# Two transformer blocks with cross-attention on one core: where the maxima's rows, the split of the feed-forward weights, the gate's first fills and the end's transfers stand

## What is computed

```python
h1 = ln(x);  x = attn(h1, h1, q1, k1, v1) @ o1 + x
h2 = ln(x);  x = attn(h2, context, q2, k2, v2) @ o2 + x     # 1601 context tokens
h3 = ln(x);  a, g = split(h3 @ ff_w1 + b1)
x = (a * gelu(g)) @ ff_w2 + b2 + x
```

## Time and profile before

| | |
|---|---|
| median of 3 runs | 3553.37 us (3542.58 to 3559.33) |
| profiled execution | 3536.07 us |
| its span of instructions | 3534.3 us |
| PE busy | 3118.4 us (88%) |
| DVE, ACT, POOL busy | 58%, 54%, 18% |
| granted clock of PE, mean | 0.936 |

### The profile page before, as it was taken

How to read it: one execution, slowest core, us unless ns; L and a number is a source line. 1 busy time by engine, 2 the same in 40 slices (tenths; PEclk the granted TensorE clock), 3 DMA queues, 4 the chain that set the end, 5 groups by cost and what they waited for, 6 DMA issues and landing times.

```text
span 3534.3 us, 43638 instructions
## 1 busy us (share of the span) xinstructions
PE 3118.4 (88%) x16000; PEld 1407.7 (40%) x16000; DVE 2057.6 (58%) x2725; ACT 1903.0 (54%) x3646; POOL 621.8 (18%) x675
## 2 busy tenths in 40 slices
PE   5687888899899998989999898898999998999978
PEld 2242333334344333534345343453434443444435
DVE  5456556767656666556656565565765675567411
ACT  1453556656564566555664565645666465646621
POOL 2222121312202031021210223101130013001010
PEclk8797888999999999999999998999999999999979
DMA  5433434432432334332433345333243214312202
GB/s 145 126 106 93 111 89 124 129 107 60 132 97 82 93 95 121 92 111 68 105 108 98 105 118 155 105 93 107 58 139 95 73 35 139 88 42 67 68 18 75
DMA packets 206357, 342.19 MB, mean 97 GB/s; under 512 B 20984, under 2 KB 105856, under 8 KB 204864
## 3 DMA queue, kind: packets, MB, share of 16 engines
q1 hardware_dynamic: 206144, 339.40, 34.9%
HBM read 202.29 MB, written 114.75 MB: 90 GB/s over the span
## 4 chain that ended last, share of the span: by engine, by line
PE 63%; DVE 10%; DMA 7%; ACT 6%; SPq 6%; issue 3%; POOL 3%; DVEq 0%; ACTq 0%; POOLq 0%
PE pr L1229 14%; PE po L1246 13%; DVE mx L1047 7%; PE pd L1216 7%; PE pf L1159 5%; PE pf L1170 5%; PE pf L1106 4%; PE pf L1147 4%; PE pf L1129 3%; ACT ET L973 3%; SPq L675 3%; PE pf L1138 2%; DMA scr_k<-HS 2%; DMA QS<-MT 2%; PE pf L1162 2%
## 5 line engine op out<-in xcount | busy, mean ns | idle before, releaser
L973 ACT ACTIVATE ET<-pr 128x512 f32<-128x512 f32 (+1 forms) x2720 | 1478.3, 597 | 1362.2 <-PE pr L1229 1347.0
L1047 DVE TENSOR_REDUCE mx<-pd 128x2 f32<-128x800 f32 (+2 forms) x1600 | 1609.9, 1031 | 987.4 <-PE pd L1216 983.7
L1229 PE MATMUL pr<-QS,KS 64*128 64x512 f32 (+1 forms) x2720 | 869.9, 510 | 157.6 <-DMA QS<-MT 79.5
L1216 PE MATMUL pd<-KS,QS 64*128 64x400 f32 (+2 forms) x3200 | 699.5, 381 | 102.3 <-DVE mx L1047 82.8
L1246 PE MATMUL po<-ET,V 128*32 128x512 f32 (+2 forms) x5440 | 758.5, 632 | 0.5 <-ACT OU L979 0.5
L1229 PEld LDWEIGHTS pr<-QS,KS 64*128 64x128 f32 (+1 forms) x2720 | 336.5, 187 | 1026.9 <-ACT ET L973 697.5
L1216 PEld LDWEIGHTS pd<-KS,QS 64*128 64x128 f32 x3200 | 385.6, 195 | 178.7 <-DVE mx L1047 135.8
L864 POOL TENSOR_TENSOR HS<-uT,HS 128x512 fp32r<-128x512 f32 (+4 forms) x168 | 190.3, 1133 | 725.4 <-ACT uT L937 725.4
L880 POOL TENSOR_TENSOR OA<-OA,DEN 128x512 f32<-128x512 f32 (+1 forms) x48 | 60.9, 1270 | 1089.5 <-DVE DEN L1055 1089.5
L1159 PE MATMUL pf<-HS,WS 128*128 128x512 f32 x730 | 211.0, 419 | 38.5 <-DVE uT L1040 22.9
L1246 PEld LDWEIGHTS po<-ET,V 128*32 128x32 f32 (+2 forms) x5440 | 107.6, 109 | 218.7 <-issue 199.5
(11 more groups left out here) (78 smaller groups left out, 2013.6 us busy)
## 6 DMA issues: line engine op xcount, KB each, us to landing
WS<-parts SPq DMA_DIRECT2D x160, 320.0 KB, 2.9
QS<-scr_q SPq DMA_DIRECT2D x80, 512.0 KB, 5.7
scr_k<-HS SPq DMA_DIRECT2D x144, 200.0 KB
scr_q<-HS SPq DMA_DIRECT2D x96, 256.0 KB
KS<-scr_k SPq DMA_DIRECT2D x80, 300.8 KB, 5.2
KS<-scr_k SPq DMA_DIRECT2D x80, 300.0 KB, 6.1
KS<-scr_k SPq DMA_DIRECT2D x80, 192.0 KB, 4.7
scr_k<-HS SPq DMA_DIRECT2D x48, 256.0 KB
```

The costliest lines, as they stand in the source:

```text
L973: activation(ET[0:q.rows[k], s % 2, 2 * pair + e, :], pr[e][0:q.rows[k], :], ACT.Exp).then_inc(score_free, 1)
L1047: v.reduce_max(mx[q.kind][:, t, 2 * p:2 * p + 2, c], pd[no % 2][:, :, 0:cols], AX_X).then_inc(unit_free, 1)
L1216: ins = mm(pd[no % 2][:, e, 0:cols], queries[:, t * P:(t + 1) * P], keys, start=True, stop=True)
L1229: mm(pr[e][0:m, :], keys, queries, start=True, stop=True).then_inc(score_ready, 1)
```

## The change

Parts, in the order of the diff:

1. The last two ff2 fills of item 6 go behind the last step, one before and one after the wait for the last group's sums (`BEHIND_BACK`); `TAIL` begins with them.
2. The split of layer 1's `ff_w1` ("w") is spread over two phases, c = 3 and c = 4, and there over the first 12 fills only, about one a step; before it was spread over all of phase c = 4.
3. At the end o2 and n3 alternate. The last n3's normalising and the last t3's subtraction go from POOL to DVE.
4. In the first two phases moves, reciprocals and divides stand 1 to 4 beats earlier.
5. Queries and keys are fetched two beats further behind their store (`STAGE_BEHIND`).
6. The second and third a fill of each gate of items 0 to 6 take `pr[0]` and `pr[1]` (`GATE_BANK`); the scores of that beat then wait for DVE's product.
7. `LAST_UNIT_AHEAD` 6 to 7, `PUT_BEHIND` 3 to 0.5.
8. One semaphore for each sequence's load of x.
9. `DEN` is moved before `OA`; POOL's multiply is in four parts, each behind its own reciprocal, and o1, o2 wait for their own part.
10. t3's first copy on ACT waits for two of the three split tiles' stores, the second for the third; g's first fill waits for h's high part, and only behind five matmuls for its low part.

```diff
-        seq = places("ff2", c - 2) + ...
+        rest = rest[:len(rest) - BEHIND_BACK]
...
-        if c % B == 0:
-            seq = mixed(seq, places("w", c // B))
+        if c == 0:
+            seq = mixed(seq, places("w", 0))
+        if c in (B - 1, B):
+            half = places("w", 1, 0, FM + 1) if c == B - 1 else places("w", 1, FM + 1)
+            easy = 3 * TT
+            seq = mixed(seq[:easy], half) + seq[easy:]
...
-BEHIND = (places("o2", N - 1) + places("n3", N - 1) + places("t3", N - 1) + ...
+BEHIND_BACK = 2
+BEHIND = ([p for t in range(TT) for p in (("o2", N - 1, t), ("n3", N - 1, t))] + places("t3", N - 1) + ...
...
-MOVE_ALONE, INVERT_ALONE, DIVIDE_ALONE = 6, (9, 10, 11, 12), 13
+MOVE_ALONE, INVERT_ALONE, DIVIDE_ALONE = 5, (8, 8, 9, 9), 10
+STAGE_BEHIND = 3
...
+PLACES[BEATS + MOVE - 1] = [("ff2", N - 2, TT - 2)]
+PLACES[BEATS + DIVIDE] = [("ff2", N - 2, TT - 1)]
...
-TAIL = FILL["o2", N - 1, 0]
+GATE_BANK = {FILL["a", i, m]: m - 1 for i in range(N - 1) for m in (1, 2)}
+GATE_BEATS = {BEAT_OF["gelu", i, 0]: i for i in range(N - 1)}
+TAIL = FILL["ff2", N - 2, TT - BEHIND_BACK]
...
-LAST_UNIT_AHEAD, PUT_BEHIND, MOST_UNITS = 6.0, 3.0, 2
+LAST_UNIT_AHEAD, PUT_BEHIND, MOST_UNITS = 7.0, 0.5, 2
...
-                  _stored + STORE + 1 if _stored >= 0 else FIRST_BEAT)
+                  _stored + STORE + STAGE_BEHIND if _stored >= 0 else FIRST_BEAT)
...
 # move_rows
+                sp.dma_start(DEN[q.kind][to, :], repeated(OU[:, :], 2 * DH, DH, DH)).then_inc(moved, 16)
                 for h in range(HG):
                     sp.dma_start(OA[q.kind][...], OU[32 * h:32 * h + DH, :]).then_inc(moved, 16)
-                sp.dma_start(DEN[q.kind][to, :], repeated(OU[:, :], 2 * DH, DH, DH)).then_inc(moved, 16)
...
 # divide, on POOL
-                pool.wait_ge(inverted, len(INVERT) * (slots_inverted(q) + 1))
-                gp.tensor_tensor(rows, rows, DEN[q.kind][0:64 * (q.g % 2) + 64, :], ALU.mult).then_inc(divided[q.kind], 1)
+                for part in range(TT):
+                    pool.wait_ge(inverted, TT * done + part + 1)
+                    gp.tensor_tensor(own, own, DEN[q.kind][rows, part * P:(part + 1) * P], ALU.mult).then_inc(divided[q.kind], 1)
...
 # t3, on ACT
-                        if f == 0:
-                            for own, count in stored_through(SPLITS_BEFORE[stage, i, f]):
-                                act.wait_ge(own, count)
+                        split = SPLITS_BEFORE[stage, i, f]
+                        for j in range(split - SPLIT_RING, split):
+                            if j % SPLIT_RING in ((0, 1), (2,), ())[f]:
+                                act.wait_ge(stored[j % SPLIT_RING], STORED[j])
...
 # n1's first wait, on DVE
-                    if i == 0:
-                        dve.wait_ge(x_first, 16)
-                    elif i < B:
-                        dve.wait_ge(x_in, 16 * (B - 1))
+                    if i < B:
+                        dve.wait_ge(x_in[i], 16)
...
+            def normalise_last(t):
+                no, b = LN0["n3", N - 1], (N - 1) % B
+                dve.wait_ge(rstd_done, TT * no + t + 1)
+                v.tensor_scalar(HN[:, t, :], X[:, b, t, :], mv[:, no % 2, t, 0:1], rstd[:, no % 2, 1, t:t + 1],
+                                ALU.subtract, ALU.mult).then_inc(norm_done, 1)
...
 # feed_forward, on PE
                 if stage == "g" and m == 0:
-                    pe.wait_ge(h_low, KC * (i + 1))
+                    pe.wait_ge(h_high, KC * (i + 1))
...
+                if stage == "g" and m == 0:
+                    pe.wait_ge(h_low, KC * (i + 1))
...
 # beside, on PE
+                if no in GATE_BANK:
+                    pe.wait_ge(score_free, HG * (beat // 4) + 2)
+                elif no - 1 in GATE_BANK:
+                    pe.wait_ge(fill_free, no - len(GATE_BANK) // (N - 1))
...
 # scores, on PE
+                if pair and 4 * s + 1 in GATE_BEATS:
+                    pe.wait_ge(fill_free, FILL["a", GATE_BEATS[4 * s + 1], 2] + 1)
```

More of the change, by code:

```diff
@@ L821, in _ @@
             sp.wait_ge(small_in, 16 * 2 * L)
-            sp.wait_ge(x_first, 16)
-            sp.wait_ge(x_in, 16 * (B - 1))
+            for own in x_in:
+                sp.wait_ge(own, 16)
         @block.gpsimd
@@ L1172, in feed_back, with beside @@
                 return ins
-            def beside(stage, i, f):
+            def beside(beat, stage, i, f):
                 if stage not in STAGE:
@@ L1252, in _ @@
                 for p in PLACES.get(beat, []):
-                    beside(*p)
+                    beside(beat, *p)
                 if beat == FIRST_BEAT:
```

47 lines of the change are left out of this document (31 added, 16 removed).

## The result

The changed kernel takes **3447.06 us** (median of 4 runs, 3441.43 to 3455.06). The kernel before took 3548.48 us beside it (4 runs, 3542.58 to 3559.33). The ratio is 0.9712, 95% interval 0.9679 to 0.9746: 2.9% faster. The forecast was 3428 with a range of 3375 to 3490. By the profiled executions, against which the prediction was added up, the forecast (3411) is 44 us too low; by the medians it is 19 too low. Stretches whose instructions are the same in two kernels differ by 2 to 6 us from one execution to the next, so a smaller difference in a single one says nothing.

A forecast was written before the change was run, and what follows sets the result against it. PE bounds the kernel, losing time idle (416 us) and at its lower clock. Terms of −106, cut to nine tenths, with −27 make −125: 3411 against the profiled 3536.1, or 3428 as a median; range 3375 to 3490.

The forecast's parts named there:

- Rival A: SP waits for maxima earlier, holding up moves and stores for DVE and ACT: −70 becomes −15, total 3478; chance 0.13.
- Maxima sent sooner: Eleven PE waits for maxima rows: −45 us, keeping 0.7 or 2 us each, plus −25 from the clock; −70.
- Rival C: SP parked at the 48 moves that feed reciprocals stops PE each time, making the kernel slower: 3633 us; chance 0.04.
- Gate: Seven gates: with three banks for the a fills, the fourth starts 2.6 us sooner each; −18 us.
- Rival D: The gate's banks do nothing, since the third a fill's chunk is late: +18, 3446 us; chance 0.05.
- First g fill: Five PE waits for h's low part, each 1.3 us shorter plus 0.9 us for the low clock; −11 us.
- End: Two ff2 fills fill PE's wait behind the last step, o2 starts sooner and warm, o2 and n3 alternate; −27 us.
- First two phases: Keys' store ahead of SP's wait for queries, −8 us; o1 and what follows four beats sooner, −3; −11 us.
- Split: Spreading ff_w1's split over two phases: 24.5 us given back, eighteen tile cycles of 6.2 us instead; +4 us.
- Rival B: The split binds at 7.4 us a tile cycle, with the clock down through twenty steps: 3459 us; chance 0.08.
- At nothing: Costed at zero: POOL's multiply in four pieces, `DEN` ahead of `OA`, and the fetch two beats later.
- Nine tenths: Discount on the −106 us beside attention, to −95 to −98, because a removed wait often uncovers a smaller one.

The follow-up runs named there:

- experiment 1: The kernel before with only the two numbers of the maxima's send changed (7.0 and 0.5): 3548.99 us, ratio 1.0011.
- 2: The changed kernel with the old two numbers of the maxima's send (6.0 and 3.0): 3455.57 us, ratio 0.9746.
- experiment 5: The changed kernel with the gate's two extra banks taken away: 3463.82 us, ratio 0.9758.
- experiment 6: The changed kernel with the two ff2 fills put back among the last steps: 3455.16 us, ratio 0.9736.
- experiment 7: The changed kernel with the fetch two beats sooner again (STAGE_BEHIND 1), which moves 7 of 200 fetches: 3466.74 us, ratio 0.9766.
- experiment 4: The changed kernel with the split of ff_w1 spread over the whole phase of item 4 again: 3448.39 us, ratio 0.972.
- experiment 12: The changed kernel with four of eighty moves, those between maxima and fetch at the start of cross phases, issued by GpSimd (POOL): 3422.08 us, ratio 0.9646.
- experiment 9: The changed kernel with all moves of sums and outputs issued by GpSimd (POOL) instead of SP: 3462.17 us, ratio 0.9756.

## Why the prediction was right, and where it was not

*Time and sign.* Right: 2.9% faster, inside the range, 19 us above the forecast. That it came so near is partly luck. The prediction's sum is −125 against the profiled execution, and the profiled executions differ by 81. Rival A's sum, −75, is nearer to that than the forecast's. The median came nearer to the forecast because the distance between the profiled execution and the median, taken as 17.3 us once and for all, was −8 in the changed kernel. The mean clock rose to 0.948 in the profiled execution and to 0.951 to 0.953 in the others, less than the 0.96 forecast. Of the phases named as signs, item 2's took 400.3 us (395 forecast), item 5's 392.6 (390) and item 6's 292.2 (415); the last never fitted, since that phase took 292.7 before the change.

*Maxima sent sooner, −70.* This is the term that failed. It is worth 0 (experiment 1) to −9 (2), outside its own bounds of −35 and −95. Each step about the waits themselves held: sends that wait for DVE alone, 56 us of waits gone, the clock at 1.00 where it was 0.50. In the second phase it brought 6 to 7 of its 11 us, and where eight of the other ten waits stood 43 to 50 us. What failed is "I keep 2 us each": the argument asked what stands behind SP at its new wait and counted DVE's cover alone. It should have followed the queue two entries further. Behind the send stand move, stores and the next self group's fetch, and the cover of that fetch, "the 2 or more steps until its first unit", was made up in part by the very wait that the change removes. A unit came to wait 6 us at a boundary and 1.8 to 3.4 us inside a phase, and each of the five at the boundaries has its own slow stretch behind it. This is rival A, which had 0.13 and a price of −15 for the term; its mechanism and nearly its price are what happened. Its total of 3478, a median, did not come; as a sum against the profiled execution (3461) it is 6 us off. Its sign, "DVE's waits for `DEN` past 80 us", did not come either (28.4 us; 71.6 with the edit alone): PE waited for fetches more than DVE for moves. Rival C, slower than before, did not come. PE's idle time, 345 us, stayed below the 370 that would have spoken against the forecast.

The rule of the Trainium skill that the prediction set aside ("TensorE: Matmul & The Clock Gate", "Terms": throttled time counts as loss whether or not PE works in it) would have added up to 29 us to this term, and so to its error. The wait above is such a stretch without work at a lower granted clock (0.64), but no run here shows it costing more than its 6.67 us and the slow work behind it.

*Gate, −18.* Right: 16.8 by undoing it, with the spacing of the fills at item 0's gate as worked out, though the gates share it unevenly (experiment 5). Rival D is out.

*First g fill, −11.* Partly. The wait of the earlier trace rows is 1.30 us now, and this kind of wait went from 12.6 to 8.9 us, of which 3.7 belong to the end's fill, which before stood in another line. That is 7 us; it was not tried alone.

*End, −27.* Right: −27.5, of which experiment 6 puts some 8 on the two ff2 fills. Their parts were other ones: 5.4 us among the steps, where 8.8 were forecast. From the last product to the first g fill are 27.2 us (46.2 before, forecast 28); its row:

```profile
3370.63 2.47 PE L1197 MATMUL pf<-HS,WS 128*128 128x512 f32 x5 [3.65 <-issue]
```

*First two phases, −11.* Right: −24, where this term and the maxima's 11 us of the second phase make −22. The 8 us for the fetch are shown by experiment 7. The second phase gained 15.3: 4 to 7 by the stages, where 3 were forecast, 6 to 7 by the maxima; the rest is open.

*Split, +4.* Right within what can be measured (experiment 4). Rival B is out: a mean cycle of 5.95 us, one of eighteen above 7.4, and the clock over the two phases that share the split is 0.95 and 0.96, where the one without had 0.96. The swing of the clock that the Trainium skill warns of ("TensorE: Matmul & The Clock Gate", "A second HAM failure mode") did not come from these steps.

*At nothing.* POOL's multiply in four pieces (453 ns each, 192 times) leaves POOL at 18%, as forecast. The fetch's beat was not nothing: it is the first phase's −8.4, which the prediction has as its −8 in another place. In the later phases it is nothing because it moves no fetch there. The move's order, the semaphores of x and t3's copies were not tried alone.

*Nine tenths.* A general discount of 8 to 11 us stood in for the question of what each removed wait had covered. It was not needed by the terms that held, and far too small for the one that failed.

## What to carry to other kernels

When a wait of the tensor engine is removed, list the transfers that were still on their way during it: what was hidden in it becomes the next wait. A wait put earlier into an in-order queue that issues all transfers costs what stands behind it, to the next deadline, so read that queue on to the next item somebody waits for. Before trusting a large term, look where the queue itself is parked (here at the send for 460 us instead of 235, at no more waiting in all). And before an edit of a table is called tested, count which entries it changes: here one that seemed to move every fetch moved 7 of 200. The cure can be as small as four moves on another queue, or leaving the old order at just the places where a deadline follows.

## What the runs showed of the hardware that was not expected

- Issuing is not a fixed cost. Four `OA<-OU` transfers took SP 4.82 us at the boundary above and 2.93 us at 1552.47 of the same trace; six stores took 5.9 to 6.2 us at the four boundaries of the changed kernel and 6.6 to 8.3 at the same four where POOL was issuing five transfers beside them (experiment 12). Part of what is taken off a queue comes back as slower issue of the rest.
- POOL issues the same four in 1.93 us, but at three of the four boundaries they land later: from the first issue of the five to the last landing are 5.6, 8.3, 11.6 and 8.9 us (experiment 12), against 5.8, 6.0, 6.8 and 5.9 from SP. Over all eighty moves the median is 6.5 (experiment 9) against 5.9. At the boundary shown, DVE's first reciprocal follows POOL's first issue by 11.7 us (1528.21 to 1539.88). From SP they were 6.9 us in the changed kernel, 1537.47 to this row:

```profile
1544.33 1.76 DVE L1093 RECIPROCAL DEN<-DEN 64x128 f32<-64x128 f32 x2 [1.09 <-DMA OA<-OU]
```

- A wait of 6.67 us is followed by 6.8 us at a mean clock of 0.60, one of 3.82 us (experiment 12) by 6.8 us at 0.75, and one of 0.77 us by none at all (the clock stays at 1.00). It does not go by length alone: behind the 5.20 us of the earlier trace rows stand 6.8 us at 0.50, and behind the changed kernel's 6.17 us (phase of item 2) 6.8 us at 0.73. That cutting a long wait into shorter ones gives time back beyond the waits themselves is suggested by this and not shown.
